# First attention layer: the partial last source tile packed three times into one tile, and column means from a sum of normalised rows

## The chip, the cores and the metric

The kernel runs on one core of one Trainium2 chip. Its time is the device time of one execution in microseconds (us); lower is better. TensorE multiplies matrices, VectorE, ScalarE and GpSimd work on rows and elements, and SyncE (SP) issues most transfers.

## The reference, cut to what matters

Four layers over a graph of N = 2708 nodes with D = 512 features and a dense adjacency matrix. Only the first is touched by the change:

```python
h = jnp.maximum(_layernorm(x, axis=-1), 0.0)
# layer 0: ALPHA = 0.2, h below is inp
hW = inp @ W
Wh1, Wh2 = hW @ a[:F_out, :], hW @ a[F_out:, :]
e = jax.nn.leaky_relu(Wh1 + Wh2.T, ALPHA)
mask = adj > 0
attention = jax.nn.softmax(jnp.where(mask, e, NEG_INF), axis=1)
negative_attention = -jax.nn.softmax(jnp.where(mask, -e, NEG_INF), axis=1)
h_prime_double = jnp.concatenate([attention @ inp, negative_attention @ inp], axis=1)
x = x + jax.nn.elu(h_prime_double @ wtrans)
```

A row whose mask is empty gets the plain mean over all nodes, so the kernel also needs the column means of h @ wtrans (first half less second half).

## The kernel before, in words

P = 128 rows make a tile; N gives T = 22 tiles, and the last of them holds LAST = 20 rows, the rest being padding. The first layer has two stages, divided by a barrier of all engines.

**prep0** loads x and the weights, and for each of the 22 row tiles normalises (moments and shift on VectorE, square root and `normalise` on ScalarE, giving h), transposes h on TensorE into the PSUM tile tp (`transpose`), splits it into a high and a low 16-bit part (`high` on ScalarE, `split` on VectorE) and multiplies it by both halves of wtrans and by two vectors (`products`, `split_product`: three products for each of four chunks, high by high, high by low, low by high). The result z = h @ wtrans, 1024 columns, is kept as z_hi (`finish`, ScalarE, line 388) and z_lo (`low`, VectorE, line 536), and two columns u and v (`dots`). The helper `pipeline` writes these steps out so that each engine is some tiles ahead of the next. Between the tiles VectorE also prepares the weights of the second layer (`bias_products`, `centre`, `dot_columns`, `rest_1`: lines 494 to 521). GpSimd (`add`, line 460) adds z_hi and z_lo of each tile to zsum, 128 x 1024. At the end u and v are transposed and stored (lines 447, 547, 364).

**attention0** works in IB = 11 blocks of 256 target rows (q = 0, 1: two halves of 128), and in each goes over the 22 source tiles j; the unit m = 22 ib + j. Per unit: ScalarE makes r (line 665); VectorE the scores of both signs (`scores`, line 762); ScalarE the exponentials (lines 673, 674); VectorE the masked weights pm (`mask`, line 774); ScalarE their high part p_hi (`high`, line 680); VectorE the low part p_lo (`low`, line 781, one unit later); TensorE for each half and sign three products of 512 columns with z (lines 942, 943, 946) and two one-column products with ones for the row sums (line 925). Buffers hold 2 units of r, 3 of scores, 2 of exponentials, 3 of pm and 5 of p_hi and p_lo. TensorE's order is by unit and half, except for the first two units of a block, whose first halves stand before the second ones. At the last tile the row sums of the second half are taken with the first half's, so that `denominator` (VectorE, lines 788 and 791) can start before the second half's products end; it stands in VectorE's program at the second unit of the next block. After it come two passes of ScalarE (`minus`, line 700) and VectorE (`evacuate`, line 800).

Beside this VectorE finds for the next block the extremes of v over each row's mask (`extreme`, lines 823, 830; eight passes of 1.6 us a block, at units 3 to 13), makes the row shifts of them (`shifts`, unit 14), and SP sends these through DRAM and back as rows (`spread`, lines 609, 614) before the next block's first `scores`, which stands at unit 20. The mask comes in two halves of 11 tiles (`load_mask`, line 601), is converted to 16 bits by ScalarE (`convert`, line 689) and stored for later layers. Before the first block VectorE does four pairs of extremes; after the second pair it makes the column means cd (`column_means`, lines 867, 869) from two products of zsum with ones (line 963). The extremes wait for the row of v, loaded 128-fold by SP (line 626).

## Time and profile before

| what | value |
|---|---|
| time, median of 3 (lowest, highest) | 2771.67 us (2769.56, 2774.1) |
| profiled execution, its own time | 2767.0 us |
| span in it | 2765.2 us |
| mean granted clock of TensorE | 0.963 |
| busy share: TensorE, VectorE, ScalarE, GpSimd | 91%, 72%, 63%, 4% |
| prep0 | start to about us 174 |
| first attention, first to last product | us 204 to 894 |

Times in rows are in us from the start of the span. A timeline row gives start, length, engine, line, operation, output and input; in square brackets stands how long the engine had been idle before and what released it. A matmul's length is longer than its distance to the next, since they overlap; the distance of two starts is its price.

### The profile page before, as it was taken

To read this page: it belongs to the slowest core of one execution; us is meant where nothing else is said; L and a number is where in the kernel's file an instruction comes from. 1 tells how busy PE (TensorE), PEld (TensorE's weight loads), DVE (VectorE), ACT (ScalarE), POOL (GpSimd) and SP (SyncE) were. 2 spreads that over 40 slices of the span, in tenths; PEclk is the share of its full clock that TensorE was granted. 3 is DMA by queue.
4 is the path that set the end of the run, shared out by engine and by line. 5 is a ranking of instruction groups with operands and counts; after the bars stand their busy time and mean duration, and the time that the engine had idled before them with its cause. 6 is when DMAs were issued, how large, how long until landed. Compare 5 with 4: busy or idle time off the path is not lost. (4 is left out here: it accounts for less than half of the span.)

```text
span 2765.2 us, 54779 instructions
## 1 busy us (share of the span) xinstructions
PE 2528.9 (91%) x20925; PEld 1564.0 (57%) x20925; DVE 1996.3 (72%) x3772; ACT 1732.1 (63%) x3143; POOL 108.3 (4%) x69
## 2 busy tenths in 40 slices
PE   7959999999999759999999995759997979999999
PEld 4424444444444439999999994324445745555554
DVE  6858999999996669999999986452236624455674
ACT  3438888888886558988888885851125544444542
POOL 3640000000000000000000000000000000000000
PEclk9979999999999889999999997979999989999999
DMA  4023344433331454111111115012111143334452
GB/s 175 29 103 124 135 137 138 157 127 126 130 125 64 153 171 158 38 38 40 38 30 37 37 28 210 1 46 68 63 63 47 38 127 96 112 109 127 123 138 51
DMA packets 182980, 259.45 MB, mean 94 GB/s; under 512 B 95717, under 2 KB 124501, under 8 KB 177001
## 3 DMA queue, kind: packets, MB, share of 16 engines
q1 hardware_dynamic: 177001, 227.71, 25.8%
q10 hardware_dynamic: 5760, 28.84, 3.3%
q8 instruction: 135, 2.21, 0.4%
q14 instruction: 84, 0.69, 0.1%
HBM read 198.17 MB, written 58.35 MB: 93 GB/s over the span
## 5 line engine op out<-in xcount | busy, mean ns | idle before, releaser
L1551 PE MATMUL m_acc<-m_y,m_b 128*128 128x260 f16 x3872 | 659.0, 275 | 21.7 <-DVE m_b L1346 21.4
L1554 PE MATMUL m_acc<-m_y,m_at 128*128 128x130 f16 x3872 | 657.8, 222 | 0.0
L1313 ACT ACTIVATE m_above<-m_u,m_nvs 128x512 bf16<-128x512 f32 (+1 forms) x864 | 519.7, 682 | 51.9 <-DVE m_b L1346 51.2
L1551 PEld LDWEIGHTS m_acc<-m_y,m_b 128*128 128x128 f16 x3872 | 376.5, 97 | 80.1 <-DMA m_at<-at 20.9
L1554 PEld LDWEIGHTS m_acc<-m_y,m_at 128*128 128x128 f16 x3872 | 381.0, 98 | 0.0
L942 PE MATMUL m_acc<-keep_z_hi,m_p_hi 128*128 128x512 f16 x968 | 365.6, 378 | 11.8 <-DVE m_p_lo L781 8.7
L943 PE MATMUL m_acc<-keep_z_lo,m_p_hi 128*128 128x512 f16 x968 | 366.0, 378 | 0.0
L946 PE MATMUL m_acc<-keep_z_hi,m_p_lo 128*128 128x512 f16 x968 | 365.0, 377 | 0.0
L1346 DVE TENSOR_TENSOR m_b<-m_above,m_at 128x1024 f16<-128x1024 bf16 (+1 forms) x432 | 280.2, 654 | 37.3 <-PE m_acc L1554 23.3
L1927 PE MATMUL m_hi<-keep_xs_hi,keep_at_first 128*128 128x512 f16 x484 | 183.5, 379 | 40.2 <-SPq L1912 32.8
L680 ACT ACTIVATE m_p_hi<-m_pm 128x512 f16<-128x512 f32 x242 | 150.9, 623 | 95.4 <-DVE m_pm L774 87.8
L762 DVE TENSOR_TENSOR m_sc<-m_r,m_g_row 128x512 f32<-128x512 f32 x242 | 166.9, 690 | 27.7 <-DMA m_g_row<-part 23.9
L1928 PE MATMUL m_lo<-keep_xs_lo,keep_at_first 128*128 128x512 f16 x484 | 183.9, 380 | 0.0
L2369 PE MATMUL m_acc<-keep_s_lo,m_wT_hi 128*128 128x512 f16 (+1 forms) x484 | 183.5, 379 | 0.0
L2368 PE MATMUL m_acc<-keep_s_hi,m_wT_hi 128*128 128x512 f16 (+1 forms) x484 | 183.5, 379 | 0.0
L2370 PE MATMUL m_acc<-keep_s_hi,m_wT_lo 128*128 128x512 f16 (+1 forms) x484 | 183.5, 379 | 0.0
L2562 ACT ACTIVATE m_lw<-m_sc 128x512 f32<-128x512 f32 (+3 forms) x70 | 32.1, 467 | 224.1 <-DVE m_mx L2413 195.3
L781 DVE TENSOR_TENSOR m_p_lo<-m_pm,m_p_hi 128x512 f16<-128x512 f32 x242 | 166.6, 689 | 6.1 <-ACT m_p_hi L680 6.0
L774 DVE SCALAR_TENSOR_TENSOR m_pm<-m_e,m_at 128x512 f32<-128x512 f32 x242 | 166.8, 689 | 3.4 <-ACT m_e L674 0.7
L942 PEld LDWEIGHTS m_acc<-keep_z_hi,m_p_hi 128*128 128x128 f16 x968 | 92.8, 96 | 134.3 <-DVE m_p_lo L781 16.9
L157 PE MATMUL p_main<-p_w_hi,p_hT_hi 128*128 128x512 f16 x352 | 138.8, 394 | 23.1 <-DVE p_hT_lo L1746 15.1
L925 PE MATMUL m_rowsum<-keep_ones,m_p_hi 128*128 128x1 f16 x968 | 159.2, 166 | 0.0
(332 smaller groups left out, 5190.9 us busy)
## 6 DMA issues: line engine op xcount, KB each, us to landing
m_at<-adjT SPq DMA_DIRECT2D x22, 1408.0 KB, 8.3
keep_a_rows<-adj ACTq DMA_DIRECT2D x40, 704.0 KB, 4.4
at<-m_at SPq DMA_DIRECT2D x22, 704.0 KB, 3.8
keep_at_first<-at SPq DMA_DIRECT2D x22, 704.0 KB, 4.0
m_at<-at SPq DMA_DIRECT2D x5, 2816.0 KB, 17.2
m_u<-rows SPq DMA_DIRECT2D x40, 256.0 KB, 3.8
low<-m_lw SPq DMA_DIRECT2D x32, 256.0 KB, 5.2
p_x_all<-x SPq DMA_DIRECT2D x4, 1536.0 KB, 14.8
```

The source lines that it names most:

```text
L942: pe.matmul(to, hi, z_hi[:, j, of], start=(j == 0), stop=False, skip_group_check=True)
L943: last = pe.matmul(to, hi, z_lo[:, j, of], start=False, stop=False, skip_group_check=True)
L946: last = pe.matmul(to, lo, z_hi[:, j, of], start=False, stop=(j == T - 1), skip_group_check=True)
L1313: act.activation(pair(above, a % RA, nb)[:, i], u[:, g % RU, 0:nb], ACT.Relu, bias=nvs[:, k, 2 * p + i:2 * p + i + 1], scale=STEEP).then_i ...
L1346: dve.tensor_tensor(to, pair(above, a % RA, nb), at[:, i0:i0 + nb, 2 * p:2 * p + 2, :].rearrange("p n j c -> p j n c"), ALU.min).then_inc( ...
L1551: pe.matmul(full.rearrange("p l y e -> p (l y e)"), pair(b01, (m // 2) % RB, nb)[:, m % 2, q // 2, half], y12[:, k % 2, j].rearrange("p l ...
L1554: last = pe.matmul(full[:, :, 1, :], at[:, i0 + q // 2, j, half], y2[:, k % 2, j], start=False, stop=(j == T - 1), skip_group_check=True)
L1927: pe.matmul(hi[:, q, :], a, xs_hi[:, j, :], **ends)
L1928: pe.matmul(lo[:, q, :], a, xs_lo[:, j, :], **ends)
L2368: pe.matmul(acc[0:r, b, :], wT_hi[:, b, k, 0:r], s_hi[:, k, :], start=(k == 0), stop=False)
L2369: pe.matmul(acc[0:r, b, :], wT_hi[:, b, k, 0:r], s_lo[:, k, :], start=False, stop=False)
L2370: last = pe.matmul(acc[0:r, b, :], wT_lo[:, b, k, 0:r], s_hi[:, k, :], start=False, stop=(k == T - 1))
```

## The change

1. Attention: the last source tile's 20 rows stand three times in the tile, at partitions 0, 32 and 64. The mask's last tile is loaded three times (20 rows each), the rest of the tile is zero; the columns of v for this tile and rows of z are copied once, so that z_hi's tile 21 holds z_hi, z_lo, z_hi. p_hi is computed in all three; VectorE then subtracts in place on partitions 64 to 127, so the tile holds high, high, low. One product stands for three, and one row sum for two, its vector of ones being 1, 0, 1 for the three parts.
2. prep0: GpSimd adds h (512 columns, 32 bits) in place of z_hi and z_lo. TensorE sums hsum over partitions, spread over 128 columns, at the end; it is split and multiplied by wtrans as a row tile is, and VectorE makes cd of it there. `column_means` and its products leave the attention. `normalise` waits for the add of two tiles before.
3. SP waits for the row of v before it loads the first mask half, and for GpSimd's zeros before the second; then follow eight copies.

Without the lists of semaphores and the renamed waits for them (`at_in[1]` counts 64 a block, not 16):

```diff
-        z_hi, z_lo, uv, zsum = keep["z_hi"], keep["z_lo"], keep["uv"], keep["zsum"]
+        z_hi, z_lo, uv, cd = keep["z_hi"], keep["z_lo"], keep["uv"], keep["cd"]
+        hsum, ones32 = kit.sb("hsum", [D]), kit.sb("ones32", [P])
...
-                for ring in (lo_done, prod_done, z_lo_done, uv_done):
+                for ring in (lo_done, prod_done, z_lo_done, uv_done, hsum_made):
...
                     act.wait_ge(tp_ready, free(t))
+                    act.wait_ge(hsum_made, free(t))
                     act.activation(h[:, b, :], flat(x_all[:, ds(t, 1), :]), ACT.Relu,
                                    bias=nmr[:, b:b + 1], scale=rstd[:, b:b + 1]).then_inc(h_ready, 1)
...
+                act.wait_ge(hs_ready, 1)
+                act.wait_ge(prod_done, done(T - 2))
+                act.activation(hT_hi[:, 0], tp[:, 1], ACT.Copy).then_inc(hs_hi, 1)
...
+                pe.wait_ge(hsum_made, done(T - 1))
+                pe.wait_ge(lo_done, done(T - 1))
+                for k in range(KC):
+                    last = pe.matmul(tp[:, 1, k, :], hsum[:, k * P:(k + 1) * P], ones32[:], start=True, stop=True, skip_group_check=True)
+                last.then_inc(hs_ready, 1)
                 pe.wait_ge(uv_done, done(T - 1))
                 pe.transpose(tp[0:2 * T, 0, 0, :], uv[:].rearrange("p s t -> p (s t)"), keep["ident"][:]).then_inc(uvt_ready, 1)
+                pe.wait_ge(hs_lo, 1)
+                pe.wait_ge(z_lo_done, done(T - 2))
+                for half in range(2):
+                    last = split_product(pe, main[:, 0, half * D:(half + 1) * D], hT_hi[:, 0], hT_lo[:, 0], w_hi[:, half], w_lo[:, half], slice(0, D))
+                last.then_inc(cs_ready, 1)
 
             @block.gpsimd
             def _(pool):
-                pool.memset(zsum[:], 0.0).then_inc(zero_made, 1)
+                pool.memset(ones32[:], 1.0)
+                pool.memset(hsum[:], 0.0).then_inc(zero_made, 1)
                 pool.wait_ge(zero_made, 1)
 
                 def add(t, b):
 
-                    wait_count(pool, z_lo_done, done(t), gate)
-                    for n, part in enumerate((z_hi, z_lo)):
-                        if n == 1 or not isinstance(t, int) or t > 0:
-                            wait_count(pool, zsum_made, 2 * t + n, gate)
-                        pool.tensor_tensor(zsum[:], zsum[:], flat(part[:, ds(t, 1), :]), ALU.add).then_inc(zsum_made, 1)
+                    wait_count(pool, h_ready, t + 1, gate)
+                    wait_count(pool, hsum_made, t + 2, gate)
+                    pool.tensor_tensor(hsum[:], hsum[:], h[:, b, :], ALU.add).then_inc(hsum_made, 1)
...
+                dve.wait_ge(hs_hi, 1)
+                dve.tensor_tensor(hT_lo[:, 0], tp[:, 1], hT_hi[:, 0], ALU.subtract).then_inc(hs_lo, 1)
                 dve.wait_ge(uvt_ready, 1)
                 dve.tensor_copy(uvT[0:2 * T, :], tp[0:2 * T, 0, 0, :]).then_inc(uvt_copied, 1)
+                dve.wait_ge(cs_ready, 1)
+                dve.tensor_scalar(cd[:], main[:, 0, D:2 * D], 1.0 / (WS * N), None, ALU.mult).then_inc(cd_made, 1)
+                dve.wait_ge(cd_made, 1)
+                dve.scalar_tensor_tensor(cd[:], main[:, 0, 0:D], 1.0 / (WS * N), cd[:], ALU.mult, ALU.subtract).then_inc(cd_made, 1)
...
+        ones_packed = kit.sb("ones_packed", [1], F16)
+        COPIES = (0, 32, 64)
...
-                    sp.dma_start(at32[:, half], dram["adjT"][ib, :, js(half), :]).then_inc(at_in[half], 16)
+                    if half == 0:
+                        sp.dma_start(at32[:, 0], dram["adjT"][ib, :, js(0), :]).then_inc(at_in[0], 16)
+                    else:
+                        sp.dma_start(at32[:, 1, 0:HJ - 1], dram["adjT"][ib, :, HJ:T - 1, :]).then_inc(at_in[1], 16)
+                        for r0 in COPIES:
+                            sp.dma_start(at32[r0:r0 + LAST, 1, HJ - 1], dram["adjT"][ib, 0:LAST, T - 1, :]).then_inc(at_in[1], 16)
...
+                sp.wait_ge(rows_in, 16)
                 load_mask(0, 0)
+                sp.wait_ge(blank_made, 1)
                 load_mask(0, 1)
+                sp.wait_ge(v_made, 3)
+                for r0 in COPIES[1:]:
+                    for of in (keep["v08"], keep["v02"], negv):
+                        sp.dma_start(of[r0:r0 + LAST, T - 1:T], of[0:LAST, T - 1:T], allow_slow_non_contiguous=True).then_inc(v_packed, 16)
+                for r0, part in zip(COPIES[1:], (z_lo, z_hi)):
+                    sp.dma_start(z_hi[r0:r0 + LAST, T - 1, :], part[0:LAST, T - 1, :]).then_inc(z_packed, 16)
...
-                pool.memset(ones32[:], 1.0).then_inc(ones_made, 1)
                 pool.memset(sign[:, 0, :], 1.0)
                 pool.memset(sign[:, 1, :], -1.0)
                 pool.memset(one[:], 1.0).then_inc(set_up, 1)
+                pool.wait_ge(set_up, 1)
+                for n, (r0, r1, value) in enumerate(((0, 32, 1.0), (32, 64, 0.0), (64, P, 1.0))):
+                    pool.memset(ones_packed[r0:r1, :], value).then_inc(ones_made, 1)
+                    pool.wait_ge(ones_made, n + 1)
+                pool.memset(at16[:, 1, HJ - 1], 0.0)
+                pool.memset(at32[:, 1, HJ - 1], 0.0).then_inc(blank_made, 1)
...
+                    if m == T - 1:
+                        act.wait_ge(v_packed, 96)
...
-                    last = act.activation(at16[:, half, part], at32[:, half, part], ACT.Copy)
+                    if j == T - 1:
+                        act.wait_ge(blank_made, 1)
+                    r = slice(0, P if j < T - 1 else 32)
+                    last = act.activation(at16[r, half, part], at32[r, half, part], ACT.Copy)
...
-                    dve.tensor_tensor(p_lo[:, m % RP], pm[:, m % RM], p_hi[:, m % RP], ALU.subtract).then_inc(lo_made, 1)
+                    if m % T < T - 1:
+                        dve.tensor_tensor(p_lo[:, m % RP], pm[:, m % RM], p_hi[:, m % RP], ALU.subtract).then_inc(lo_made, 1)
+                    else:
+                        low = p_hi[COPIES[2]:P, m % RP]
+                        dve.tensor_tensor(low, pm[COPIES[2]:P, m % RM], low, ALU.subtract).then_inc(lo_made, 1)
...
-                def column_means():
-                    dve.wait_ge(zs_made, 1)
-                    dve.tensor_scalar(cd[:], acc[:, 2, 1], 1.0 / N, None, ALU.mult).then_inc(cd_made, 1)
-                    dve.wait_ge(cd_made, 1)
-                    dve.scalar_tensor_tensor(cd[:], acc[:, 2, 0], 1.0 / N, cd[:], ALU.mult, ALU.subtract).then_inc(cd_made, 1)
...
-                    if c == 1:
-                        column_means()
...
-                    return pe.matmul(rowsum[:, ib % 2, 2 * q + s:2 * q + s + 1], part, ones[:, 0:1],
-                                     start=(j == 0 and q == 0 and s == 0 and lo == 0), stop=(j == T - 1 and lo == 1), skip_group_check=True)
+                    return pe.matmul(rowsum[:, ib % 2, 2 * q + s:2 * q + s + 1], part, (ones if j < T - 1 else ones_packed)[:, 0:1],
+                                     start=(j == 0 and q == 0 and s == 0 and lo == 0), stop=(j == T - 1), skip_group_check=True)
...
+                    if m == T - 1:
+                        pe.wait_ge(z_packed, 32)
+                        pe.wait_ge(ones_made, 3)
                     pe.wait_ge(lo_made, m + 1)
                     for s in range(2):
                         to = acc[:, n % 3, s]
                         hi, lo = (part[:, m % RP, s, q * P:(q + 1) * P] for part in (p_hi, p_lo))
                         of = slice(s * D, (s + 1) * D)
-                        pe.matmul(to, hi, z_hi[:, j, of], start=(j == 0), stop=False, skip_group_check=True)
-                        last = pe.matmul(to, hi, z_lo[:, j, of], start=False, stop=False, skip_group_check=True)
-                        if not (j == T - 1 and q == 1):
-                            sums(ib, j, q, s, 0)
-                        last = pe.matmul(to, lo, z_hi[:, j, of], start=False, stop=(j == T - 1), skip_group_check=True)
-                        if not (j == T - 1 and q == 1):
-                            last = sums(ib, j, q, s, 1)
+                        last = pe.matmul(to, hi, z_hi[:, j, of], start=(j == 0), stop=(j == T - 1), skip_group_check=True)
+                        if j == T - 1:
+                            continue
+                        pe.matmul(to, hi, z_lo[:, j, of], start=False, stop=False, skip_group_check=True)
+                        sums(ib, j, q, s, 0)
+                        pe.matmul(to, lo, z_hi[:, j, of], start=False, stop=False, skip_group_check=True)
+                        last = sums(ib, j, q, s, 1)
                     if j == T - 1 and q == 0:
-                        for s in range(2):
-                            for half in range(2):
-                                last = sums(ib, j, 1, s, half)
+                        for qs in range(4):
+                            last = sums(ib, j, qs // 2, qs % 2, 0)
...
-                pe.wait_ge(ones_made, 1)
-                for s in range(2):
-                    last = pe.matmul(acc[:, 2, s], ones32[:], zsum[:, s * D:(s + 1) * D], start=True, stop=True, skip_group_check=True)
-                last.then_inc(zs_made, 1)
                 pe.wait_ge(wide_made, 1)
-                pe.wait_ge(cd_made, 2)
```

## Rows read from the trace of the kernel before

**Rows 1.** Windows of two stages: stretch, length, busy us (instructions) of each engine, clock, DMA

```profile
0.00:150.00 150.00, 127.43 (x805) 68.65 (x806) 111.29 (x204) 56.16 (x92) 77.96 (x41) 0.99 0.27 97
...
455.00:518.00 63.00, 62.33 (x443) 29.92 (x441) 59.19 (x100) 53.66 (x119) 0.00 (x0) 1.00 0.41 137
```

**Rows 2.** Timeline of TensorE at the last tile: start us, length us, line, operation

```profile
515.24 0.38 PE L942 MATMUL m_acc<-keep_z_hi,m_p_hi 128*128 128x512 f16 x1
...
515.45 0.38 PE L943 MATMUL m_acc<-keep_z_lo,m_p_hi 128*128 128x512 f16 x1
...
515.69 0.38 PE L946 MATMUL m_acc<-keep_z_hi,m_p_lo 128*128 128x512 f16 x1
...
516.74 0.38 PE L942 MATMUL m_acc<-keep_z_hi,m_p_hi 128*128 128x512 f16 x1
...
518.49 0.38 PE L942 MATMUL m_acc<-keep_z_hi,m_p_hi 128*128 128x512 f16 x1 [0.30 <-PE m_acc L946]
```

**Rows 3.** What line 788 (denominator) waits for: releaser, us in total, times

```profile
  PE m_rowsum L925: 23.2, 11
```

**Rows 4.** Timeline of VectorE at the denominators of three blocks

```profile
454.28 0.16 DVE L788 SCALAR_TENSOR_TENSOR m_den<-keep_iso,m_rowsum 128x4 f32<-128x4 f32 x1 [1.35 <-PE m_rowsum L925]
...
516.91 0.16 DVE L788 SCALAR_TENSOR_TENSOR m_den<-keep_iso,m_rowsum 128x4 f32<-128x4 f32 x1 [0.98 <-PE m_rowsum L925]
...
892.37 0.16 DVE L788 SCALAR_TENSOR_TENSOR m_den<-keep_iso,m_rowsum 128x4 f32<-128x4 f32 x1 [11.25 <-PE m_rowsum L925]
```

**Rows 5.** Timeline of TensorE and VectorE inside one block

```profile
495.67 0.39 PE L942 MATMUL m_acc<-keep_z_hi,m_p_hi 128*128 128x512 f16 x1 [0.36 <-DVE m_p_lo L781]
...
507.48 0.69 DVE L762 TENSOR_TENSOR m_sc<-m_r,m_g_row 128x512 f32<-128x512 f32 x1 [2.18 <-DMA m_g_row<-part]
...
515.24 0.69 DVE L781 TENSOR_TENSOR m_p_lo<-m_pm,m_p_hi 128x512 f16<-128x512 f32 x1
```

**Rows 6.** Groups of instructions by line, to us 180: GpSimd's adds of the low halves

```profile
L460 POOL TENSOR_TENSOR keep_zsum<-keep_zsum,keep_z_lo 128x1024 f32<-128x1024 f32 x22 | 48.6, 2207 | 5.2 <-POOL keep_zsum L460 5.2
```

**Rows 7.** Timeline of prep0, several engines

```profile
32.78 1.01 ACT L388 ACTIVATE keep_z_hi<-p_main 128x1024 f32 x1
...
48.46 1.78 DVE L113 SCALAR_TENSOR_TENSOR p_nmr<-p_mv,p_rstd 128x1 f32<-128x1 f32 x1
...
51.52 0.38 PE L157 MATMUL p_main<-p_w_hi,p_hT_hi 128*128 128x512 f16 x1 [2.29 <-DVE keep_z_lo L536]
...
83.47 1.79 DVE L510 TENSOR_TENSOR p_w<-p_wt,p_w 128x512 f32<-128x512 f32 x1
...
104.09 0.38 PE L157 MATMUL p_main<-p_w_hi,p_hT_hi 128*128 128x512 f16 x1 [2.08 <-DVE keep_z_lo L536]
...
138.59 1.01 ACT L388 ACTIVATE keep_z_hi<-p_main 128x1024 f16<-128x1024 f32 x1
...
144.54 1.01 ACT L388 ACTIVATE keep_z_hi<-p_main 128x1024 f16<-128x1024 f32 x1
```

**Rows 8.** Window of two microseconds in prep0

```profile
106.00:108.00 2.00, 2.00 (x7) 0.66 (x5) 1.85 (x4) 0.00 (x0) 1.76 (x2) 0.50 0.57 65
```

**Rows 9.** Timeline of VectorE in the attention's tail

```profile
894.76 0.75 DVE L800 SCALAR_TENSOR_TENSOR m_y<-m_acc,m_den,m_o 128x512 f32<-128x512 f32 x1 [0.24 <-ACT m_o L700]
```

**Rows 10.** Timeline at the end of prep0 and the attention's first work

```profile
166.11 1.02 ACT L388 ACTIVATE keep_z_hi<-p_main 128x1024 f16<-128x1024 f32 x1 [4.46 <-PE p_small L159]
...
168.30 0.27 DVE L547 COPY p_uvT<-p_tp 44x128 f32<-44x128 f32 x1
...
171.17 2.12 POOL L460 TENSOR_TENSOR keep_zsum<-keep_zsum,keep_z_lo 128x1024 f32<-128x1024 f32 x1 [0.24 <-POOL keep_zsum L460]
...
180.78 1.62 DVE L830 CUSTOM_DVE_ANT_0 m_dropped<-m_v_row,keep_am 128x1408 bf16<-128x1408 f32 x1 [6.07 <-DMA m_v_row<-rows]
```

**Rows 11.** Timeline of VectorE at the column means

```profile
187.43 0.69 DVE L867 TENSOR_SCALAR m_cd<-m_acc 128x512 f32<-128x512 f32 x1
...
188.76 1.61 DVE L830 CUSTOM_DVE_ANT_0 m_dropped<-m_v_row,keep_am 128x1408 bf16<-128x1408 f32 x1
```

More of the change, by code:

```diff
@@ L315, in prep0 @@
         (w_hi_made, w_lo_made, wa_hi_made, wa_lo_made, am_made, gate, a_in, wa_made, wa_copied, h_ready, tp_ready, hi_ready, lo_done, prod_done, z_hi_done,
-         z_lo_done, uv_done, uvt_ready, uvt_copied, rows_out, zsum_made, zero_made) = kit.sems(
+         z_lo_done, uv_done, uvt_ready, uvt_copied, rows_out, hsum_made, zero_made, hs_ready, hs_hi, hs_lo, cs_ready, cd_made) = kit.sems(
             "w_hi_made w_lo_made wa_hi_made wa_lo_made am_made gate a_in wa_made wa_copied h_ready tp_ready hi_ready lo_done prod_done z_hi_done "
-            "z_lo_done uv_done uvt_ready uvt_copied rows_out zsum_made zero_made")
+            "z_lo_done uv_done uvt_ready uvt_copied rows_out hsum_made zero_made hs_ready hs_hi hs_lo cs_ready cd_made")
         w1 = wt
@@ L560, in attention0 @@
         a_rows, am, dropped = keep["a_rows"], keep["am"], kit.sb("dropped", [HN], BF16)
-        ones32 = kit.sb("ones32", [P])
         vx, top, sign, one = kit.sb("vx", [2, 2, 2]), kit.sb("top", [2, 2]), kit.sb("sign", [2, 2]), kit.sb("one", [1])
         s1, s2, g = kit.sb("s1", [2, 2]), kit.sb("s2", [2, 2]), kit.sb("g", [2, 2])
-        negv, cd = kit.sb("negv", [T]), kit.sb("cd", [D])
+        negv, cd = kit.sb("negv", [T]), keep["cd"]
         r, sc, e, pm = kit.sb("r", [RR, BW]), kit.sb("sc", [RS, 2, BW]), kit.sb("e", [RE, 2, BW]), kit.sb("pm", [RM, 2, BW])
         p_hi, p_lo = kit.sb("p_hi", [RP, 2, BW], F16), kit.sb("p_lo", [RP, 2, BW], F16)
+        ones_packed = kit.sb("ones_packed", [1], F16)
+        COPIES = (0, 32, 64)
         y, o, x = kit.sb("y", [2, D]), kit.sb("o", [2, D]), kit.sb("x", [2, D])
@@ L570, in attention0 @@
         rowsum = kit.ps("rowsum", [2, 512])
-        z_hi, z_lo, zsum = keep["z_hi"], keep["z_lo"], keep["zsum"]
+        z_hi, z_lo = keep["z_hi"], keep["z_lo"]
         ones, iso, uv = keep["ones16"], keep["iso"], keep["uv"]
@@ L576, in attention0 @@
          den_made, rden_made, o_made, y_made, iso_made, elu_made, plus_made, x_made, am_made, max_made, min_made, ext_link,
-         g_made, cd_made, zs_made, ones_made, wide_made, turned, g_first) = kit.sems(
+         g_made, wide_made, turned, g_first, blank_made, v_packed, z_packed, ones_made) = kit.sems(
             "rows_in x_in x_out g_out set_up v_made r_made sc_made e_made pm_made hi_made lo_made p_used acc_made "
             "den_made rden_made o_made y_made iso_made elu_made plus_made x_made am_made max_made min_made ext_link "
-            "g_made cd_made zs_made ones_made wide_made turned g_first")
+            "g_made wide_made turned g_first blank_made v_packed z_packed ones_made")
         DEN_AT, EVACUATE_AT, ISO_AT, PLUS_AT, FINISH_AT = 1, (2, 4), (15, 16), 18, 20
@@ L685, in convert @@
                     if part == 0:
-                        act.wait_ge(at_in[half], 16 * (ib + 1))
+                        act.wait_ge(at_in[half], (16, 64)[half] * (ib + 1))
                         if ib > 0:
                             act.wait_ge(at16_out[half], 16 * ib)
-                    last = act.activation(at16[:, half, part], at32[:, half, part], ACT.Copy)
+                    if j == T - 1:
+                        act.wait_ge(blank_made, 1)
+                    r = slice(0, P if j < T - 1 else 32)
+                    last = act.activation(at16[r, half, part], at32[r, half, part], ACT.Copy)
                     if part == HJ - 1:
@@ L768, in mask @@
                     if part == 0:
-                        dve.wait_ge(at_in[half], 16 * (ib + 1))
+                        dve.wait_ge(at_in[half], (16, 64)[half] * (ib + 1))
                     dve.wait_ge(e_made, m + 1)
@@ L2633, in build @@
             keep |= {"z_hi": kit.sb("z_hi", [T, 2 * D], F16), "z_lo": kit.sb("z_lo", [T, 2 * D], F16),
-                     "uv": kit.sb("uv", [2, T]), "zsum": kit.sb("zsum", [2 * D]),
+                     "uv": kit.sb("uv", [2, T]), "cd": kit.sb("cd", [D]),
                      "a_rows": kit.sb("a_rows", [2, NP // 2]), "am": kit.sb("am", [2, NP // 2], BF16),
```

## Prediction

> **What bounds the kernel now.** I read the stage windows first. The preparation of the first layer (prep0, to about us 174) keeps TensorE busy 85% of its first 150 us, and in a block of 256 rows of the first attention TensorE is busy 62.3 of 63.0 us with VectorE close behind at 59.2 [rows 1]. So a saved matmul is not simply a saved matmul: the question is who is late next.
>
> TensorE's timeline around the last source tile gives its prices. Matmuls of 512 columns start 0.215 us apart, a one-column row sum costs about 0.025, so a group of three products and two sums takes 0.70 us. The last tile's first half begins at 515.24 and its second at 516.74, 1.50 us with the four extra sums; the next block starts at 518.49 [rows 2].
>
> Then VectorE's wait for these row sums. It stops for them at the top of every block: 23.2 us in 11 waits [rows 3], of which the last, with nothing behind it, is 11.25. That leaves 11.95 in ten, 1.35 and 0.98 in two neighbours [rows 4]. It is the one wait of VectorE on TensorE. The other direction: TensorE's margin to VectorE's low parts shrinks while VectorE also searches extremes, and at tile 14, start 495.67, it has run out (0.36 us idle). VectorE also waits about 2.2 us a block for the row maxima that come back by DMA, and its low part that precedes the denominator starts at 515.24 and ends at 515.93 [rows 5]. So the block of 62.63 us (454.28 to 516.91) closes in a loop: denominator, VectorE without a pause to tile 14, TensorE without a pause from tile 14 through the first half of tile 21, denominator. Beside it VectorE alone, with its DMA wait, needs 62.63 less 0.98 = 61.65 us.
>
> Last, prep0. GpSimd adds two halves of 1024 elements per row tile, 44 adds of 2.2 us; the 22 of the low half are 48.6 us, the others as much [rows 6]. While one runs, VectorE instructions with two SBUF inputs stretch: one of a single element takes 1.78 us, one of 512 elements 1.79, where its like takes 0.69 elsewhere [rows 5, 7]. TensorE pays with waits for the low part of z, as the 2.29 us before 51.52. A row tile takes 5.95 us where nothing disturbs (138.59 to 144.54), and 17 tiles (32.78 to 144.54) take 111.76 where 17 x 5.95 is 101.15: 10.6 us are lost [rows 7]. Part of it is clock: after the idle time before 104.09 the granted clock falls to 0.50, and some eight products run at half speed, 8 x 0.215 = 1.7 us [rows 7, 8].
>
> **The change part by part.** The sum is made against the profiled execution (span 2765.2, its own time 2767.0 us); the median shown, 2771.67, is 4.7 above that, and I move it by the same difference.
>
> *Last tile, blocks.* Of each of four groups two products and one sum go: 2 x 0.215 + 0.025 = 0.455 us, 1.82 a block, 20.0 over 11 blocks if TensorE alone set the time. It doesn't. The first half of the tile shrinks from 1.50 to 0.53 us (two products, four sums, small ends), 0.97 less, so the row sums come 0.97 earlier and VectorE's wait of 0.98 goes to about nothing. The loop falls to 62.63 - 0.97 = 61.66, level with VectorE's own 61.65. The 0.86 saved in the second half only makes TensorE wait for the low part of tile 1 and again at tiles 10 to 14. Ten blocks at 0.95, since some waits may be a little shorter than the one shown: -9.5 us. Bounds: 0 (VectorE takes it all back) and -20.0.
>
> *The last block and its tail.* No successor's row maxima weigh on VectorE there (it waits 11.25 us at the end), so TensorE sets the pace: it enters about 0.76 earlier and saves 0.97 to the denominator. From the sums, 0.17 us before the denominator at 892.37, to the second evacuation at 894.76 pass 2.56 us [rows 4, 9]; with the second half at 0.43 us the order is denominator, two ScalarE passes of 0.7 to 0.8 back to back, evacuation, 2.25. Together -2.0; bounds -1.0 and -2.7.
>
> *Mask pieces, packed copies, waits in the attention.* The second half mask comes in four DMAs in place of one, three more issues in SP's queue per block, right after the previous block's last mask is used and some 30 us before tile 11 needs it; the maxima's round trip is issued 40 us behind them. The eight copies of small columns and z rows once in block 0 are needed at tile 21, about 60 us later. VectorE's low part of the last tile covers half the partitions with the same 512 elements, so the same 0.69; ScalarE's conversion likewise. Zero; bounds 0 and +0.4 a block, +4, should DMAs hold back the maxima, since VectorE waits for them.
>
> *GpSimd in prep0.* 44 adds of 1024 become 22 of 512 elements, about 1.1 us each by half of one of 2.2: 97 to 24 us. They follow the normalised tile, right behind ScalarE; the stretched weight work of VectorE stands behind its low part of z, at another point of the tile. Without the stretch VectorE's extra work between two tile pairs (some 3.5 us uncontended) fits in the slack of 2 x 5.95 us. ScalarE's new wait asks for the add of two tiles earlier, 1.1 in 5.95 us: never late. The first adds now fall into the start, us 19 to 28, where VectorE splits weights: up to +1. I take -9.0 of the 10.6; bounds -10.6 and 0.
>
> The Trainium skill ("SBUF — State Buffer", section "SBUF: two separate sides") says that VectorE with two SBUF inputs and GpSimd lock a shared pair of ports for a whole instruction and the loser fully blocks. The 1.78-us instruction above agrees. By that rule the 22 new adds block as well, only for less time; it is the second rival.
>
> *End of prep0.* Now GpSimd's last add ends it: start 171.17, end 173.29 [rows 10]. New chain: ScalarE's last z_hi runs 166.11 to 167.13 and VectorE's last low part ends at 168.30; the four column-sum matmuls and ScalarE's copy hide under these. Then VectorE's subtraction, 0.69, to 169.0; 24 products x 0.215 = 5.2, 0.2 to drain, to 174.4; two VectorE passes as those of 187.43 to 188.76, 1.33 [rows 11], to 175.75. That is +2.5 us. TensorE idles some 2.2 us before the 24 products. A like gap before 51.52 left the next product at 0.38 us, the full clock; the one before 104.09 cost 1.7 [rows 7, 8]. I take half, +0.9; bounds 0 and +5.2 (all 24 at half clock).
>
> *Start of the attention.* The column means leave VectorE's chain of extremes, on which the first product hangs: -1.33 [rows 11]. The row of v was waited for until 180.78 [rows 10] and now has the DMA queues to itself, the masks waiting behind it: 0 to -0.7, I take 0. The first mask half, loaded some 6 us later, is needed 20 us after the row of v lands: hidden.
>
> Sum: -9.5 - 2.0 + 0 - 9.0 + 2.5 + 0.9 - 1.3 = -18.4 us; 2771.67 - 18.4 = **2753.3 us**.
>
> **The rivals.**
> 1. VectorE keeps the attention's time. For: its own loop, 61.65 us, is only 0.98 below the block. Against: that 0.98 is just what the shorter half tile returns. If ScalarE or the maxima then run late instead, the 9.5 goes: 2762.8.
> 2. prep0 does not recover: 22 adds still collide, at half an add (0.55 us) each 12 us of VectorE time, or the TensorE idle time has another cause. For: GpSimd's adds now sit beside the shift chain, and two-input instructions are many. Against: the tile pairs have slack for it. Then the 9.0 goes: 2762.3.
> 3. TensorE alone sets the block: 20.0 in place of 11.5, 2744.8. For: it is busy 99%. Against: the 0.36-us wait at tile 14.
> 4. Slower: the clock. TensorE will idle about 2 us a block in pieces, and the gap before 104.09 was followed by half clock at a price of 1.7 us. If every block takes such dips between tile 14 and 21, on the loop, one per block costs 17 and cancels the gain; from 1.1 per block the kernel is slower, at two it is 2753.3 + 34 = 2787. Against: the new gaps are under 1 us each, and the present ones of 0.3 to 0.4 leave the clock whole.
> 5. The order of dependences makes the change do less than it says, both 1 and 2: 2771.8, no change.
>
> **How the numbers follow.** Forecast 0.62 (own range 2749 to 2758); rival 1 0.10; rival 2 0.14; rival 3 0.05; rival 4 0.03; rival 5 0.06. About 5.5 us, 0.2%, is what the measurement can tell: below 2766.1 is faster, above 2777.2 slower. The range 2746 to 2764 holds the forecast and rivals 1 and 2, and leaves out 0.14. Forecast and rivals 1 to 3 are faster, 0.91, rival 5 the same, rival 4 slower; with a hundredth moved for small costs I left at zero: faster 0.90, same 0.06, slower 0.04.
>
> **What would show it.** In the profile after: block period near 61.7 us and the wait before the denominator near 0 (62.6 means rival 1, 60.8 rival 3); TensorE's waits for low parts of P up by about 1 us a block; in prep0 a tile every 5.95 us, no 1.8-us VectorE instruction in the weight work, last z_hi near us 157; then 24 products with 0.38 or 0.63 us each; the attention's first product about 7 us earlier than before (-9.0 + 2.5 + 0.9 - 1.3); granted clock 1.00 in all full blocks. Wrong if the attention's span from first to last product shrinks by under 6 us, or if its first product comes less than 2 us earlier.

## The result, and the profile after

The kernel after takes 2748.24 us (median of 4 runs, 2747.92 to 2749.07), the kernel before on the same chip 2770.76 (4 runs, 2769.56 to 2774.1). The ratio is 0.9917, 95% interval 0.9904 to 0.993: 22.5 us faster, by the medians. The forecast was 2753.3, range 2746 to 2764. The profiled execution of after took 2747.92 us, its span is 2746.1, its mean granted clock 0.965. One execution of the later kernel with the row sums first took 3806.17 us at a mean clock of 0.648 and is left out of the numbers below.

The span shrinks by 19.1 us. The starts of a few instructions divide it into stages; before's are in [rows 2, 4, 7, 9 to 11], or are told in the table where no row stood. The period of a block is the distance of two denominators; a mean period is over the nine of them that lie between the first ten denominators, and the last block, with no successor, stands by itself:

| stage, us | before | after | difference | predicted |
|---|---|---|---|---|
| start to last z_hi of prep0 | 166.11 | 155.89 | -10.2 | -9.0 |
| last z_hi to issue of the row of v (174.33; 166.65) | 8.22 | 10.76 | +2.5 | +2.5, clock +0.9 |
| that to the first product (204.00; 194.47) | 29.67 | 27.82 | -1.9 | -1.3 |
| first product to first denominator | 62.18 | 61.21 | -1.0 | } -9.5 |
| first to tenth denominator, nine blocks | 564.28 | 556.22 | -8.1 | } |
| last block and tail (to 903.93; 882.83) | 73.47 | 70.93 | -2.5 | -2.0 |
| the other layers, untouched | 1861.3 | 1863.3 | +2.0 | 0 |

The windows of after, 150 us of prep0, two stretches of it, and one block (columns as in [rows 1]):

```profile
0.00:150.00 150.00, 134.60 (x867) 73.44 (x868) 97.15 (x211) 59.01 (x95) 28.91 (x29) 1.00 0.27 98
...
30.00:60.00 30.00, 30.00 (x202) 15.58 (x201) 22.94 (x52) 11.51 (x20) 7.86 (x7) 1.00 0.23 88
...
120.00:150.00 30.00, 30.00 (x205) 15.68 (x204) 14.92 (x32) 11.15 (x18) 5.06 (x4) 1.00 0.07 19
...
441.32:503.11 61.79, 60.60 (x429) 28.96 (x428) 58.99 (x99) 53.34 (x118) 0.00 (x0) 1.00 0.43 140
```

From 30 to 150 us TensorE no longer idles (30.00 of 30.00 in all four stretches of 30 us, the two not shown included); in the block it idles 1.2 us where it idled 0.7 [rows 1]: another engine is late there. The last source tile on TensorE, to be held against [rows 2]:

```profile
502.40 0.59 PE L984 MATMUL m_acc<-keep_z_hi,m_p_hi 128*128 128x512 f16 x2
502.83 0.24 PE L964 MATMUL m_rowsum<-m_ones_packed,m_p_hi 128*128 128x1 f16 x4
502.94 0.59 PE L984 MATMUL m_acc<-keep_z_hi,m_p_hi 128*128 128x512 f16 x2
503.83 0.38 PE L984 MATMUL m_acc<-keep_z_hi,m_p_hi 128*128 128x512 f16 x1 [0.30 <-PE m_acc L984]
```

The first half takes 0.54 us (502.40 to 502.94) where it took 1.50. On VectorE the block now looks so (a wait for the row maxima, the packed low part, the denominator):

```profile
494.34 0.69 DVE L806 TENSOR_TENSOR m_sc<-m_r,m_g_row 128x512 f32<-128x512 f32 x1 [1.88 <-DMA m_g_row<-part]
...
500.42 0.69 DVE L829 TENSOR_TENSOR m_p_hi<-m_pm,m_p_hi 64x512 f16<-64x512 f32 x1
...
503.11 0.16 DVE L836 SCALAR_TENSOR_TENSOR m_den<-keep_iso,m_rowsum 128x4 f32<-128x4 f32 x1
```

The denominator waits for nothing here; the two waits of a full block in [rows 4] are 1.35 and 0.98 us. Over all blocks, its line's releaser, to be held against [rows 3]:

```profile
  PE m_rowsum L964: 11.4, 2
```

11.4 us in two, of which 10.29 is the last block and 1.16 the first. What VectorE's scores wait for between 196 and 885 us:

```profile
  DMA m_g_row<-part: 22.9, 10
```

In prep0, VectorE's groups and GpSimd's adds (to be held against [rows 6, 7]):

```profile
L524 DVE TENSOR_TENSOR p_w<-p_wt,p_w 128x512 f32<-128x512 f32 x8 | 5.5, 686 | 0.1
...
L113 DVE SCALAR_TENSOR_TENSOR p_nmr<-p_mv,p_rstd 128x1 f32<-128x1 f32 x22 | 4.0, 181 | 3.4 <-DVE p_rstd L111 0.5
```

```profile
L474 POOL TENSOR_TENSOR p_hsum<-p_hsum,p_h 128x512 f32<-128x512 f32 x22 | 27.8, 1265 | 109.7 <-ACT p_h L380 86.1 <-issue 23.2 <-POOL p_hsum L474 0.4
```

And the end of prep0 and the attention's first work, in time:

```profile
155.89 1.02 ACT L390 ACTIVATE keep_z_hi<-p_main 128x1024 f16<-128x1024 f32 x1 [4.46 <-PE p_small L159]
...
158.09 0.68 DVE L561 TENSOR_TENSOR p_hT_lo<-p_tp,p_hT_hi 128x512 f16<-128x512 f32 x1
...
158.82 0.39 PE L157 MATMUL p_main<-p_w_hi,p_hT_hi 128*128 128x512 f16 x1 [1.86 <-DVE p_hT_lo L561]
...
164.94 0.69 DVE L567 SCALAR_TENSOR_TENSOR keep_cd<-p_main,keep_cd 128x512 f32<-128x512 f32 x1
...
166.65 0.37 SPq L652 DMA_DIRECT2D m_v_row<-rows  x1
```

### The profile page after: what moved, and what is told of

It is laid out like the page before. It is cut to its first block and busy times, and to the rows that moved or that the text cites. A ratio compares the mean times of both kernels' runs of the same rounds, so it can differ in the third digit from the quotient of the medians.

```text
span 2746.1 us, 54512 instructions
## 1 busy us (share of the span) xinstructions
PE 2512.3 (91%) x20821; PEld 1556.2 (57%) x20821; DVE 1978.9 (72%) x3773; ACT 1731.8 (63%) x3144; POOL 40.4 (1%) x52
## 5 line engine op out<-in xcount | busy, mean ns | idle before, releaser
L987 PE MATMUL m_acc<-keep_z_lo,m_p_hi 128*128 128x512 f16 x924 | 349.2, 378 | 0.0
L989 PE MATMUL m_acc<-keep_z_hi,m_p_lo 128*128 128x512 f16 x924 | 348.3, 377 | 0.0
L826 DVE TENSOR_TENSOR m_p_lo<-m_pm,m_p_hi 128x512 f16<-128x512 f32 x231 | 159.2, 689 | 3.3 <-ACT m_p_hi L721 3.3
L964 PE MATMUL m_rowsum<-keep_ones,m_p_hi 128*128 128x1 f16 x924 | 153.1, 166 | 0.0
```

The costliest lines, as they stand in the source:

```text
L987: pe.matmul(to, hi, z_lo[:, j, of], start=False, stop=False, skip_group_check=True)
L989: pe.matmul(to, lo, z_hi[:, j, of], start=False, stop=False, skip_group_check=True)
```

## Experiments

Each ran with the kernel before on the same chip. The first four ran on chip 14 (median of before 2769.4), the next four on chip 4 (2771.45), then two on chip 2 (2772.47) and the last two on chip 10 (2771.76); which chip the result above was taken on is not on record. This will matter for the blocks.

**Without GpSimd's adds** (kernel before):

```diff
-                    for n, part in enumerate((z_hi, z_lo)):
...
-                        pool.tensor_tensor(zsum[:], zsum[:], flat(part[:, ds(t, 1), :]), ALU.add).then_inc(zsum_made, 1)
```

> The kernel before without GpSimd's 44 adds (left out: the sum of z, so the column means are zero). Theory A, the adds block VectorE's two-input instructions and that stops TensorE: the last z_hi starts near us 156 instead of 166.1 (-10), no two-input instruction of 512 elements above 0.7 us, granted clock 1.00 in all of prep0; the stage also ends at VectorE's last work and the store of u and v, some 2 us earlier than GpSimd's last add did. Total -12 us, 2759. Theory B, the waits come from the order of VectorE's weight work, whatever GpSimd does: last z_hi stays within 2 us of 166, total -2 to -4 us.

2752.8 us, ratio 0.9938 (0.9921 to 0.9954). The last z_hi stands at 156.03, TensorE is busy 30.00 of 30.00 in the four windows, the block period is 62.62. So the adds alone cost prep0 all its idle time. The gain is above what was expected, also because the wait for the last add at the end of prep0 went (8.22 to 4.96 us), which I had left out.

**Memsets in their place** (kernel before; four a tile, 88 in all, no SBUF input):

```diff
+                    for n in range(4):
...
+                        pool.memset(zsum[:], 0.0).then_inc(zsum_made, 1)
```

> The kernel before with four memsets of 1024 elements (3.8 us a tile) in place of GpSimd's two adds (4.3 us a tile): GpSimd is nearly as busy but reads nothing (left out: the sum of z, so the column means are zero). Theory A, it is the reading of SBUF that blocks VectorE: last z_hi near us 156 and two-input instructions at 0.69 us, total about -11 us. Rival, any GpSimd instruction blocks VectorE while it runs: last z_hi near 165, two-input instructions of up to 1.6 us, total -1 to -3 us.

2756.23 us, ratio 0.9951 (0.9934 to 0.9967). GpSimd's and VectorE's groups:

```profile
L460 POOL MEMSET keep_zsum<- 128x1024 f32 x88 | 83.8, 952 | 74.0 <-DVE keep_z_lo L536 63.7 <-POOL keep_zsum L460 10.3
```

```profile
L510 DVE TENSOR_TENSOR p_w<-p_wt,p_w 128x512 f32<-128x512 f32 x8 | 5.5, 686 | 0.1
```

The last z_hi stands at 155.55, TensorE is again busy 30.00 of 30.00 in the four windows. GpSimd is busy 84 us (with the adds twice some 48 [rows 6]), and VectorE's two-input instruction keeps its 686 ns, none of 512 elements is above 693; with the adds it is 1.79 us [rows 7]. It is not GpSimd at work that stretches VectorE, but GpSimd reading SBUF. The kernel is 3.4 us slower than the one without adds since its stage still ends with GpSimd: 8.25 us from the last z_hi to the issue of the row of v, in place of 4.96.

**Each half of the change alone** (the packed last tile on the kernel before; then prep0 and the column means on it, below, with the attention's tiles as before):

```diff
+                        low = p_hi[COPIES[2]:P, m % RP]
+                        dve.tensor_tensor(low, pm[COPIES[2]:P, m % RM], low, ALU.subtract).then_inc(lo_made, 1)
...
+                        if j == T - 1:
+                            continue
```

```diff
-        z_hi, z_lo, uv, zsum = keep["z_hi"], keep["z_lo"], keep["uv"], keep["zsum"]
+        z_hi, z_lo, uv, cd = keep["z_hi"], keep["z_lo"], keep["uv"], keep["cd"]
...
-                    if c == 1:
-                        column_means()
```

> The kernel before with the packed last tile alone; GpSimd's adds and the column means stay as they were. Theory A, a loop through the denominator sets the block: block period 62.7 to 61.8 us, VectorE's wait before the denominator near 0, last block and tail 2.5 us shorter, total -11.5 us (2759). Rival, TensorE alone sets the block: period 60.8, total -20. Rival, VectorE takes it back: period 62.6, total -2.

> The kernel before with the GpSimd sum of h and the column means by a product in prep0 alone; the attention's last tile as before, masks not held back. Theory A: last z_hi near us 156 (-10), end of prep0 +2.5, attention's start -1.3, blocks of 62.7 us unchanged, total -9 us (2762). If the parts add up, this, the packed tile alone (-11.5) and the row of v served first (-0.5) give the whole change's -21 to -22.5. Rival, the parts overlap (one slack is spent twice): the sum of the two is more than 3 us above the whole.

Packing alone: 2754.8 us, 0.9943 (0.9927 to 0.996), period 61.66 to 61.78. prep0 alone: 2759.07, 0.9963 (0.9949 to 0.9977), last z_hi 155.27, period 62.62. The two gains, 14.6 and 10.3, sum to 24.9 against 22.5 for the whole, 2.4 more, where the expectation had named 3 as the sign of an overlap; as ratios, 0.9943 x 0.9963 is 0.9906, inside the whole's interval. An overlap of a us or two is neither shown nor excluded.

The profiled execution of packing alone ran prep0's old code in 136.18 us from first to last z_hi, where before's took 133.33. Each has one dip of the clock: in packing alone TensorE idles 2.66 us before 53.44 and the clock is 0.56 from 53 to 55 us, in before the dip is that of [rows 8]. So the dip isn't the difference. TensorE's six longest idle times are: 2.66, 2.68, 0.47, 2.08, 2.08 and 0.84 us in packing alone, together 10.8; 2.29, 0.77, 1.57, 2.08, 0.39 and 0.84 in before, together 7.9. That is the 2.9 us. The instructions are the same, so it seems that they met GpSimd's adds at other moments; no run isolates it.

**One half of the last tile with three products again** (kernel after; the surplus products are repeats of the first, so the output is another):

```diff
+                            if q == 1:          # the other kernel: q == 0
+                                for _ in range(2):
+                                    last = pe.matmul(to, hi, z_hi[:, j, of], start=False, stop=True, skip_group_check=True)
```

> The changed kernel with each product of the last tile's second half issued three times (its own product is added three times, so those rows of the output differ). It gives back 4 x 0.215 = 0.86 us of TensorE time a block, all of it behind the row sums. Theory A, the loop runs through the first half only: block period stays at 61.8 us, only the last block and its tail grow, +0.3 to +1, total about 2749. Rival, TensorE's own time sets the block: +0.86 x 11 = +9.5 us, 2758.

> The changed kernel with each product of the last tile's first half issued three times (the output of those rows differs). The same 0.86 us a block, now ahead of the row sums. Theory A: block period 61.8 to 62.6 us, VectorE waits 0.8 to 1.0 us before the denominator again, total +9 us, 2757. Rival, VectorE's own loop of 61.7 us sets the block and TensorE has slack: under +2 us.

Second half thrice: 2748.3, 0.992 (0.9904 to 0.9937), period 61.67, the same time as after within the noise; only the last block grows, from 60.21 to 60.95, and its tail by 0.3. First half thrice: 2755.99, 0.9948 (0.9931 to 0.9965), period 62.53. So 0.86 us in the first half is worth 0.86 us a block (62.53 less 61.67), and the same in the second half nothing in a full block: the loop runs through the first half and the denominator.

**The wait for the maxima filled** (kernel after; the last part of `finish` moves from unit 20 to unit 19):

```diff
-        DEN_AT, EVACUATE_AT, ISO_AT, PLUS_AT, FINISH_AT = 1, (2, 4), (15, 16), 18, 20
+        DEN_AT, EVACUATE_AT, ISO_AT, PLUS_AT, FINISH_AT = 1, (2, 4), (15, 16), 18, 19
```

> The changed kernel with VectorE's last step of the block before (finish, 1.15 us) at unit 19 instead of 20, where VectorE now waits 2.0 us for the row maxima: its own loop falls from 61.7 to about 60.5 us. Theory A, both loops are level now (the one through TensorE is 61.66 by the prediction's sum): period 61.8 to 61.6, total -1 to -2 us. Rival, VectorE's loop alone sets the block: period 60.7, -11 us.

2748.06, 0.9921 (0.9904 to 0.9937): no gain that can be told, where 1 to 2 us had been expected. VectorE's wait for the maxima all but goes, and the wait before the denominator comes back in its place, 1.76 us a block; the period is 61.67. That is TensorE's own loop.

**Row sums ahead of the last tile's products**, on a semaphore of their own, on top of the last edit (not shown: ScalarE's first `minus` now waits for the products itself):

```diff
-                    dve.wait_ge(acc_made, 2 * ib + 1)
+                    dve.wait_ge(sums_made, ib + 1)
...
+                    if j == T - 1 and q == 0:
+                        for qs in range(4):
+                            last = sums(ib, j, qs // 2, qs % 2, 0)
+                        last.then_inc(sums_made, 1)
```

> As the one with finish at unit 19, and the four row sums of the last tile stand before its products with a semaphore of their own, so the denominator can start 0.43 us earlier. Theory A, the loop through TensorE is the next limit: period 61.8 to about 61.2 us, total -5 to -7 us against the changed kernel, 2742. Rival, VectorE's loop alone: no more than the one with finish at 19 gives. Rival, nothing moves since ScalarE or the DMA of the maxima is late next: 2748.

2744.61 (median of three, lowest 2744.05), 0.9907 (0.9887 to 0.9927), period 61.36: 3.5 us below the wait-filled kernel on the same chip, less than the 5 to 7 expected, and the best kernel that computes all. TensorE and VectorE at one block's end:

```profile
501.58 0.24 PE L963 MATMUL m_rowsum<-m_ones_packed,m_p_hi 128*128 128x1 f16 x4
501.68 1.02 PE L987 MATMUL m_acc<-keep_z_hi,m_p_hi 128*128 128x512 f16 x4
```

```profile
501.85 0.16 DVE L835 SCALAR_TENSOR_TENSOR m_den<-keep_iso,m_rowsum 128x4 f32<-128x4 f32 x1 [1.47 <-PE m_rowsum L963]
```

The denominator starts 0.27 us behind the start of the row sums and no longer behind two products.

**Without the mean product** (kernel after; the sum over partitions, its split, 24 products and cd are left out, cd is zero), and **masks at once** (kernel after without one wait of SP):

```diff
-                last.then_inc(hs_ready, 1)
...
-                last.then_inc(cs_ready, 1)
```

```diff
-                sp.wait_ge(rows_in, 16)
                 load_mask(0, 0)
```

> The changed kernel without the column means at the end of prep0 (left out: the sum over partitions, its split, the 24 products and VectorE's two passes; cd is zero). Theory A, that chain alone is late there: from the last z_hi to the attention's first transfer 10.8 us becomes about 5.0, as in the kernel without adds; total -5 to -6 us against the changed kernel, 2743. Rival, the store of u and v is as late: -2 us or less.

> The changed kernel with SP loading the first mask half without waiting for the row of v. Theory A, the masks take DMA time from the row of v: from its issue to VectorE's first extreme 6.45 us as before, instead of 5.9. Rival, it queues ahead of them anyway: 5.9.

The first: 2750.6 (2748.76 to 2752.77), 0.9919 (0.9903 to 0.9936), where I had expected 2743. From the last z_hi to the issue of the row of v it takes 4.98 us, 5.8 less than after, as expected. But its profiled execution, at 2752.77 the longest of the four, loses that in two other places. The last z_hi comes 3.8 us later than in after (159.65): TensorE waits 2.00 us for a normalised tile before 33.00, in the start of prep0, and the clock falls (mean 0.82 and 0.84 in the two windows from 30 to 40 us). And the block period is 62.47, nine times 0.67 us more. The second, a single execution: 2752.62; from the issue of the row of v to the first extreme 6.44 us against 5.92 with the wait, so the order of the transfers is worth 0.5 (over all traces 5.9 to 6.25 us with the wait, 6.4 to 6.5 without); its period is 62.16. Neither edit touches a block. VectorE, in a block of the first:

```profile
495.05 0.69 DVE L788 TENSOR_TENSOR m_sc<-m_r,m_g_row 128x512 f32<-128x512 f32 x1 [2.65 <-DMA m_g_row<-part]
```

It waits 2.65 us for the maxima, where after waits 1.88, and not at all for the denominator. This led to two last kernels, which were taken on another chip.

**Without the mean product, the wait filled** (first line), and that with the row sums first (the lines behind it):

```diff
+        DEN_AT, EVACUATE_AT, ISO_AT, PLUS_AT, FINISH_AT = 1, (2, 4), (15, 16), 18, 19
...
+                    dve.wait_ge(sums_made, ib + 1)
...
+                        last.then_inc(sums_made, 1)
```

> The kernel after without the matmul sum of hsum and its product with wtrans (the column means are zero), with the last units of finishing the row shifts moved from unit 20 to unit 19, so that VectorE has a piece of work between issuing the row maxima and waiting for them. Theory A (the 5.8 us saved at the end of prep0 in the run without the mean product were lost again because VectorE's loop of a block holds the bare round trip of the row maxima through DRAM, which was some 0.7 us longer there): period 61.67, VectorE's wait for the rows near 0, span near 2740, time near 2743, 5 us under the kernel after. Theory B (the longer block comes from something else in that kernel, as the granted clock or the first block's order): period stays 62.3 and the time near 2750.

> The kernel after without the column-mean product (means are zero), with finish at unit 19 and the last tile's row sums ahead of its products on a semaphore of their own. Theory A (gains of the end of prep0 and of the row sums add up once the round trip is hidden): period 61.36, time near 2744.7 - 5.5 = 2739. Theory B (this kernel's round trip is longer and reappears as waits of VectorE): period 62 or more, time 2745 or more.

2742.8 (2741.21 to 2743.97), 0.99 (0.9884 to 0.9917), period 61.69, and 2740.45, 0.9892 (0.9875 to 0.9908), period 61.37: the periods and times of theory A both times. But its premise, a longer round trip in this kernel, does not show: the round trip is 13.85 and 13.79 us, not 14.45, and the wait for the maxima is not near 0. In the first of the two:

```profile
488.84 0.69 DVE L788 TENSOR_TENSOR m_sc<-m_r,m_g_row 128x512 f32<-128x512 f32 x1 [0.84 <-DMA m_g_row<-part]
...
497.51 0.16 DVE L818 SCALAR_TENSOR_TENSOR m_den<-keep_iso,m_rowsum 128x4 f32<-128x4 f32 x1 [1.12 <-PE m_rowsum L946]
```

So how much of the gain over the kernel without the mean product is the filled wait and how much the shorter round trip can't be read off. An estimate: with 13.85 us and no filling, VectorE would wait the 2.1 us of after, and the period would be 61.86; then of the 0.78 us a block some 0.2 are the filling and 0.6 the round trip.

The kernels by chip (us; wait and period are means over nine blocks). Where VectorE hardly waits for the maxima, as in the two wait-filled kernels of chip 4, the round trip can't be read and they are left out:

| kernel | chip | maxima: issue to the scores behind them | VectorE's wait for them | period |
|---|---|---|---|---|
| before | not known | 13.85 | 2.15 | 62.70 |
| after | not known | 13.76 | 2.06 | 61.80 |
| no adds | 14 | 13.26 | 1.55 | 62.62 |
| memsets | 14 | 13.18 | 1.49 | 62.62 |
| packing alone | 14 | 13.20 | 1.50 | 61.69 |
| prep0 alone | 14 | 13.38 | 1.63 | 62.62 |
| second half thrice | 4 | 13.19 | 1.46 | 61.67 |
| first half thrice | 4 | 13.08 | 1.33 | 62.53 |
| masks at once | 2 | 14.14 | 2.42 | 62.16 |
| no mean product | 2 | 14.45 | 2.73 | 62.47 |
| the same, wait filled | 10 | 13.85 | 0.98 | 61.69 |
| the same, row sums first | 10 | 13.79 | 0.94 | 61.37 |

The round trip goes with the chip, or with the moment at which the kernels of a chip ran, and hardly with the kernel: on one chip it differs by 0.3 us at most, whatever the edits, and the means of two chips by up to 1.2. No kernel was profiled on two chips, so this too is read from the table and not isolated.

In the three kernels in which VectorE sets the block (after, masks at once, no mean product), period less wait is 59.74 in the mean. So the rule for a block with the packed tile, `finish` at unit 20: the longer of 61.67 us (TensorE's loop) and 59.74 us plus the wait for the maxima (VectorE's), level at a wait of 1.93. The kernel before has such a second loop as well. Three of its nine blocks are longer than 62.63, those with the longest waits, and yet VectorE stands 0.92 us before the denominator in each:

```profile
695.68 0.69 DVE L762 TENSOR_TENSOR m_sc<-m_r,m_g_row 128x512 f32<-128x512 f32 x1 [2.49 <-DMA m_g_row<-part]
...
699.84 0.69 DVE L781 TENSOR_TENSOR m_p_lo<-m_pm,m_p_hi 128x512 f16<-128x512 f32 x1
...
705.06 0.16 DVE L788 SCALAR_TENSOR_TENSOR m_den<-keep_iso,m_rowsum 128x4 f32<-128x4 f32 x1 [0.92 <-PE m_rowsum L925]
```

```profile
700.20 0.38 PE L946 MATMUL m_acc<-keep_z_hi,m_p_lo 128*128 128x512 f16 x1
...
700.58 0.39 PE L942 MATMUL m_acc<-keep_z_hi,m_p_hi 128*128 128x512 f16 x1
```

The late low part (it ends at 700.53) holds TensorE back at tile 20: two products start 0.38 us apart where others take 0.215 to 0.24. Through TensorE's last two tiles the delay reaches the row sums, and with them the denominator. The periods of the three blocks, 62.84, 62.88 and 62.77, are 60.39 plus their waits of 2.45, 2.49 and 2.38; the other six, with waits up to 2.18, take 62.63. So before's two loops are level at a wait of 2.24.

## Why the prediction was right, and where it was off

- **The loop of a block was read rightly.** Its 61.66 us, from 62.63 less the 0.97 saved in the first half, is measured as 61.67 in two kernels (second half thrice, wait filled); the saving in the second half is worth nothing in a full block, as the prediction said. Rivals 1 and 3 fall with the same rows: the periods 62.6 and 60.8 are not there.
- **-9.5 came out as -9.0** (first product to tenth denominator). The prediction's second loop was misread. It took the whole 0.98 us before the denominator as VectorE's slack, and 61.65 as what VectorE alone needs. In the kernel before, 0.92 of that is never free: with the shown wait of 2.18 us VectorE's loop, which closes through TensorE's last two tiles, needs 60.39 + 2.18 = 62.57, and its slack was 0.06. The 9.5 came nearly whole all the same, since the change shortens this way through TensorE too. What is left is VectorE's own program: 59.47 us and the wait for the maxima by the prediction's numbers (61.65 less 2.18), 59.74 and the wait as measured. The 0.27 more are a wait for ScalarE's r near the start of six of the nine blocks (0.14 to 0.19 us, as below) and instructions that are a few ns longer each, together 0.17.

```profile
444.33 0.69 DVE L806 TENSOR_TENSOR m_sc<-m_r,m_g_row 128x512 f32<-128x512 f32 x1 [0.19 <-ACT m_r L706]
```

- **So VectorE decides in after, by little**: 59.74 + 2.06 = 61.80 against 61.67, which by the periods costs 10 x 0.13 = 1.3 us. The round trip was not longer than in before (13.76 and 13.85). But with it at 14.45, as on chip 2, the same blocks take 0.8 us more than 61.67, 8 us in all. Of the doubt "should DMAs hold back the maxima": the mask's three small pieces do not. The kernels with them have 13.08 to 13.20 us on chips 14 and 4, those without 13.18 to 13.38 on chip 14.
- **Rival 4, the clock, falls**: the granted clock is 1.00 in all ten periods of after. TensorE idles 1.07 to 1.33 us a block where it idled 0.66 to 0.73, half of the 1 us more that the prediction had named. The first product comes 9.5 us earlier (7 predicted), and the span from first to last product shrinks by 11.6, so neither sign of being wrong is there. Rival 5, both losses together, falls with rivals 1 and 2.
- **prep0, -9.0, was short by 1.2**: I took 9.0 of 10.6, and 10.2 came. Rival 2 is refuted: no two-input instruction of the weight work is stretched (686 ns); the 22 adds still collide with a few at the start, as the 1.32 us of line 496 at 27.52, at no cost that the windows behind us 30 show. My 1.1 us for an add was 1.265: half the elements took 57% of 2.207 [rows 6].
- **End of prep0: +2.5 measured, +2.5 predicted**, and of the clock's +0.9 nothing: behind 1.86 us of idle time the first of the 24 products took 0.39 us and they started 0.2155 apart, all at the clock 1.00.
- **Start of the attention: -1.3 became -1.9.** The column means gave their 1.3; the row of v, costed at 0 with bound -0.7, gave some 0.5, which the kernel with the masks at once takes back.
- **Last block and tail: -2.0 became -2.5**: 60.21 us in place of 61.91 to the denominator, 0.8 behind it.
- **Median against profile.** The profiled span shrank by 19.1, the median by 22.5. I had moved before's profile by a constant 4.7 us; but before's own executions spread over 8 us (2766.7 to 2774.76), and those of after over 1.2. That is 3.4 of the 4.1 us by which the change came out larger than the 18.4 of the sum, and the sum did not foresee it. Where the adds of z run, idle time in prep0 differs by execution, as packing alone against before shows (2.9 us), and the spread is wide; but it does not end with them: without any adds it is 0.5 us, in the kernel without the mean product 4.0 and in the two last ones 2.8 and 3.4, and the kernel without the mean product has a dip of the clock in its profile. What spreads the executions is open.
- **The 2.0 us in untouched layers** go with the new prep0: in the ten kernels that have it the rest of the program takes 1862.6 to 1864.8 us, in the four with the old one 1861.0 to 1861.3. The cause stays open; the prediction had no term for it. The first layer alone gained 21.1 us, not 18.4; that the profile's total of 19.1 lies so near the forecast is luck.

The Trainium skill ("SBUF — State Buffer", section "SBUF: two separate sides") limits the lock against a two-input VectorE instruction to GpSimd operations that read SBUF. The kernel with memsets agrees: 83.8 us of GpSimd and 686 ns on VectorE.

## What to carry to other kernels

Before a saved matmul is counted, follow the loop that closes the period: here the first half's share of the four shortened groups was worth nearly its full price in every block, and the other half something in the last block alone. An idle microsecond before a cross-engine wait is not yet slack. See what a delay of the waiting engine would do on its other ways: here its late low part held back the very engine it later waited for, and of 0.98 us only 0.06 was free. Blocks of one trace that differ in one wait show this without a new run. When two loops are within tenths of a us, a DMA round trip in one of them shows its whole variation, so give it work to hide behind; and compare kernels on one chip, or the variation between chips is taken for the edit's. A GpSimd operation that reads SBUF is priced by what it stretches on VectorE and then on TensorE, not by its own time.

## What the hardware showed unexpectedly

- GpSimd's memsets of 128 x 1024 (952 ns each, 88 of them) leave VectorE's two-input instructions at 686 ns; with adds beside them they reach 1.84 us in the kernel before.
- The same two small transfers, out to DRAM and back as rows, take 13.1 to 13.4 us on two chips, 13.8 on a third and 14.1 to 14.5 on a fourth, nearly whatever the kernel; what sets the length is open.
- A gap of about 2 us on TensorE is followed by half clock in some cases (2.08 us before 104.09; 2.66 before 53.44 in packing alone; 2.00 before 33.00 without the mean product) and not in others (2.29 before 51.52; 1.86 before 158.82 in after; 2.68 before 81.80 in packing alone).
